# A graph kernel's half stage loads 133 of a row's 325 columns

## What is computed

```python
out_i = act(jnp.concatenate([x_i, edge_attr], -1) @ W).reshape(-1, HEADS, DIM)
out_j = act(jnp.concatenate([x_j, edge_attr], -1) @ W).reshape(-1, HEADS, DIM)
alpha = act((jnp.concatenate([out_i, out_j], -1) * att).sum(-1))
mu = alpha.mean(0)
var = alpha.var(0)
alpha = (alpha - mu) * jax.lax.rsqrt(var + BN_EPS) * bn_gamma + bn_beta
alpha = act(alpha)
alpha = segment_softmax(alpha, i, N_NODES)
msg = out_j * alpha[:, :, None]
aggr = jax.ops.segment_sum(msg, i, num_segments=N_NODES)
out = aggr.mean(1) + bias
```

## Time and profile before

| | |
|---|---|
| median of 3 runs | 6269.24 us (6267.83 to 6273.7) |
| profiled execution, its own time | 6264.56 us |
| its span in the trace | 6262.9 us |
| PE busy | 4644.9 us (74%) |
| DVE busy | 4803.2 us (77%) |
| ACT busy | 3989.2 us (64%) |
| POOL busy | 3785.3 us (60%) |
| moved by DMA | 1270.97 MB |

### The profile page before, as it was taken

One profiled execution on the slowest core, in us unless ns is written; L12 is line 12 of the kernel. 1 busy time (PEld: TensorE's weight loads), 2 busy tenths in 40 slices (PEclk: granted clock), 3 DMA queues, 4 the chain that ended last, 5 costly groups with the idle time before them and its releaser, 6 DMA issues. The chain is left out here.

```text
span 6262.9 us, 166674 instructions
## 1 busy us (share of the span) xinstructions
PE 4644.9 (74%) x32887; PEld 3061.9 (49%) x32888; DVE 4803.2 (77%) x30826; ACT 3989.2 (64%) x10577; POOL 3785.3 (60%) x5381
## 2 busy tenths in 40 slices
PE   1367766777666666578988988889838888886799
PEld 0144444444343343345555555555425555554799
DVE  6588988888887788678888888888876677667233
ACT  3366666666555555478888888888867777776000
POOL 2277777777776666645555555555547777776000
PEclk8599999998888888799999999999979999998899
DMA  8767767676555555566556666556537777774798
GB/s 217 251 221 229 229 220 231 217 231 205 195 189 196 189 187 186 185 193 166 165 165 166 169 165 165 166 164 166 144 107 216 216 216 217 215 217 147 298 361 340
DMA packets 913988, 1270.97 MB, mean 203 GB/s; under 512 B 268468, under 2 KB 775459, under 8 KB 894916
## 3 DMA queue, kind: packets, MB, share of 16 engines
q1 hardware_dynamic: 785592, 864.14, 47.7%
q0 software_dynamic: 88560, 320.26, 13.8%
q10 hardware_dynamic: 39580, 84.01, 3.6%
HBM read 837.45 MB, written 430.64 MB: 202 GB/s over the span
## 5 line engine op out<-in xcount | busy, mean ns | idle before, releaser
L912 POOL DMA_INDIRECT rows<-rowS,idx x1616 | 1754.8, 1086 | 614.5 <-issue 478.3
L1632 POOL TENSOR_SCALAR one<-io128b,bufh 128x128 bf16<-128x128 bf16 x912 | 716.3, 785 | 796.2 <-DMA bufh<-rows 796.1
L1666 DVE CUSTOM_DVE_ANT_0 junk<-bufh,attb 128x64 bf16<-128x64 f32 x5472 | 1021.6, 233 | 150.3 <-ACT bufh L1714 134.2
L1172 PE MATMUL psa<-one_c,one_s 128*128 128x392 bf16 x2352 | 552.7, 347 | 733.2 <-DVE one_s L994 501.5
L2397 PE MATMUL psm<-msg,onem 128*128 128x260 f32 x3648 | 919.9, 395 | 211.5 <-issue 177.1
L2318 POOL TENSOR_TENSOR msg<-oj,heads 128x512 f32<-128x512 f32 x760 | 796.2, 1069 | 211.6 <-DMA oj<-rows 177.3
L2397 PEld LDWEIGHTS psm<-msg,onem 128*128 128x128 f32 x3648 | 648.7, 190 | 482.4 <-issue 407.4
L986 DVE TENSOR_TENSOR one_c<-ioc,pairS 128x1176 bf16<-128x1176 f16 x784 | 593.9, 757 | 245.5 <-DMA pairS<-pairs 127.2
L1754 PE MATMUL pre<-P3h,oneT 128*128 x5472 | 756.5, 274 | 0.0
L1008 DVE CUSTOM_DVE_ANT_0 weighed<-rowS,att_row 128x64 bf16<-128x64 f32 x4848 | 735.6, 214 | 7.6 <-ACT rowS L1068 7.5
L1065 ACT ACTIVATE lgS<-preS 128x1024 f32<-128x1024 f32 x404 | 413.2, 1023 | 440.1 <-PE preS L1161 439.3
(11 more groups left out here) (306 smaller groups left out, 9161.8 us busy)
## 6 DMA issues: line engine op xcount, KB each, us to landing
bufh<-rows SPq DMA_DIRECT2D x912, 325.0 KB, 3.3
oj<-rows SPq DMA_DIRECT2D x912, 256.0 KB
adj<-adj SPq DMA_DIRECT2D x70, 1568.0 KB, 9.4
adj<-cnts ACTq DMA_DIRECT2D x49, 1568.0 KB, 7.2
eaS<-in_edge_attr_dram SPq DMA_DIRECT2D x201, 256.0 KB
low<-dlow SPq DMA_DIRECT2D x202, 252.0 KB
adj_early<-adj SPq DMA_DIRECT2D x28, 1568.0 KB, 8.5
rows<-blanktail POOLq DMA_DIRECT2D x20, 1625.0 KB, 44.0
```

What stands on the lines that cost most here:

```text
L912: eng.indirect_dma_start(out=m["rows"][h], out_offset=bass.IndirectOffsetOnAxis(ap=idx[s][:, k:k + 1], axis=0), in_=rows[s][:, k, :], in_o ...
L1172: mm = eng.matmul(psa[r][:, 0:z.GC], one_s[r][:, k, :], one_c[r][:, k, :], start=(k == 0), stop=(k == GT - 1))
L1632: eng.tensor_scalar(one[j % PRE][:, 1, :], m["io128b"][:, :], buf[j][:, 1, 0, LANE:LANE + 1], 0.0, ALU.add, ALU.is_equal).then_inc(second_ ...
L1666: ins = eng.tensor_tensor_reduce(junk[q][:, k * H + h, 0, :], buf[j][:, k, 1, h * D:(h + 1) * D], attb[:, 1, h, :], 1.0, 0.0, ALU.mult, AL ...
```

## The change

The load of the half stage takes columns DOTS * D = 192 to 325 of each row in place of all 325, and puts them at the same place in the buffer. Columns 0 to 191, the first three heads of `out_j`, are left out; their dot products come with the row. The number of transfers, the semaphores, the buffers and the order of instructions on every engine stay the same, and the rows in DRAM too.

```diff
@@ -1617,7 +1617,7 @@
             def body(i, h):
                 for j in range(BU):
                     wait(eng, sp_read[j], i)
-                    eng.dma_start(buf[j][:, :, 0, :], tiles(i, j, h)).then_inc(row_in[j], 16)
+                    eng.dma_start(buf[j][:, :, 0, DOTS * D:RW], tiles(i, j, h)[:, :, DOTS * D:RW]).then_inc(row_in[j], 16)
 
             paired_parts(eng, z.its, body)
```

## The result

The changed kernel takes 6166.7 us in the median of 4 runs (6164.8 to 6175.18), the kernel before 6268.53 (4 runs beside them, 6261.71 to 6273.7). The ratio is 0.9841, 95% interval 0.9824 to 0.9858: 1.6% faster. The profiled execution took 6167.14 us of its own time (span 6165.4), 97.4 less than that of before.

What follows compares the result with a forecast made beforehand. The half stage was bound by a ring of load, POOL, PE, ACT and DVE, with one DMA latency per pass. 152 passes x 0.62 = 94 us; 6264.6 - 94 = 6170.6, set at 6173; range 6130 to 6221 us.

Steps and rivals of the forecast that it cites:

- One DMA latency per pass: Half stage: a load's 3.26 us wait lies on the path once per six-unit pass, not once per unit.
- The cut of 0.66 us: Half stage load: engine time falls from 1.21 to 0.55 us, landing to 2.6 to 2.65 us.
- the ring: Half stage: load, POOL, PE, ACT and DVE wait on each other over six buffers, 11.59 us in the pass read.
- The cap of 0.67 us or a little over: Half stage: the most a pass can give, however fast the load, before DVE's half of the one-hot decides.
- DVE's ring: Half stage: DVE's in-order sums, one-hots and reads with PE and ACT; would leave a pass of 10.92 us.
- the tie: Half stage: cut 0.66 and cap 0.67 us leave two rings level, the later deciding each time.
- The 0.62 us per pass: Half stage: gain taken per pass after cut and cap; over 152 passes 94 us.
- Rival E: Half stage: earlier POOL work slows DVE's reads, making the kernel slower, 125 us, 6390 us; 5%.
- A: Half stage load: smaller cut, 0.74 us of engine time per load, 46 to 71 us gained; 17%.
- B: Half stage: gain hidden anyway, DVE's half as late as POOL's; no change, 6264 to 6270 us; 10%.
- C: Half stage: larger cut, 0.89 us, with DVE's slack; 0.75 to 0.9 us per pass, 114 to 137 us gained; 13%.
- D: Half stage: gain partly eaten as earlier POOL work meets DVE's reads, 10 to 45 us gained; 5%.

Runs made afterwards that it cites:

- wide_early: Kernel before, full 325-column load kept; DVE reads the fourth head first, so SP issues the next load earlier: 6684.53 us against 6838.92, ratio 0.9785.
- small_early: Changed kernel (133 columns), with DVE reading the fourth head first so the load is issued earlier: 6669.85 us, ratio 0.9758 to the kernel before.
- tally: Changed kernel, with DVE making the one-hot of a pass's unit 3 ahead of adding up the old pass's sums: 6124.68 us, ratio 0.9813 to the kernel before.
- mid: Kernel before, with only the first head's 64 columns left out of the load (261 columns): 6791.64 us, ratio 0.9948.
- tiny: Changed kernel, loading only 69 columns, the fourth head's part left out and zeros in its place: 6108.65 us, ratio 0.9785 to the kernel before.

## Why the prediction was right

- **One DMA latency per pass: right.** Landing and stage time go together over four kernels that differ only in the load: 3.3 us and 1833; 3.0 and 1791; 2.5 and 1736; 2.2 and 1686. That is 147 us for 1.05 us (3.27 to 2.22 at two decimals), 0.92 us per pass for each us of landing. And wide_early gives the same kind of gain with no byte less.
- **The cut of 0.66 us: right for the ring, too small for the landing.** The engine time fell by 1.21 - 0.56 = 0.65 us, the value taken. The median landing fell by 0.74, to 2.52 and not 2.6 to 2.65. What the ring feels is POOL's start: from the issue to it the mean fell from 3.43 to 2.75 us, by 0.69. By the Trainium skill's fit (DMA: Bandwidth & Descriptors, Anatomy of one DMA) it would have been 0.45, and these runs don't bear that out: its 69 us stand against 97. The page gives that fit for transfers that GpSimd issues, which the prediction did not say; these loads are issued by SP.
- **The cap of 0.67 us or a little over: wrong as a mean.** It is true of the pass that I read, 11.59 us, one of the shortest: only 5% of the passes take 11.6 us or less. The mean pass had 12.06. The floor of DVE's ring is small_early's 1672 / 152 = 11.0 us, so the cap was 1.06 us per pass. The error was to take a cap from one pass and the gain from the mean of all. With it went the tie: the load's ring went on leading, by 0.29 us in the mean and in 94% of the passes.
- **The 0.62 us per pass: 0.636 measured, in part by luck.** The prediction took 0.66 and put off 0.04 for two tied rings. The rings did not tie. In the table the load's step gave 0.69, and small losses that the sum did not have took it back to 12.07 - 11.45 = 0.62: 0.04 in POOL's one-hot (0.79 to 0.83), 0.04 from PE's transpose to Exp, 0.02 ahead of the issue, less 0.03 in the last steps. The errors of the cut (0.03) and of the tie (0.04) met these losses (0.06).
- **Rival E's mechanism is there, but did not grow.** In the kernel before, DVE's read of one head takes 236 ns where POOL works beside nearly all of it and 215 where POOL stands still (2043 and 1872 reads in passes 10 to 149); in the changed kernel 233 and 218. POOL's one-hot of any unit took 0.72 us where no read lay beside it and 0.80 where reads lay beside more than 80% of it. So both pay a little, and neither is held up for the length of the other. This agrees with the rule that stood beside it (the Trainium skill, SBUF — State Buffer, Who interferes with whom), that this pair contends. What did grow, POOL's one-hot of unit 0, was not pushed into reads by the change, it lay among them before; why it grew stays open. It now lies beside DVE's one-hot of the same unit for 0.30 us where that was 0.06, and DVE's one-hot grew with it, from 0.25 to 0.31 us; in small_early the two don't meet and it takes 0.25, in tally they meet for 0.33 and it takes 0.34.
- **Rivals.** A is out (a load takes 0.56 us of engine time, not 0.74), B is out (mid and tiny move the time by the load alone), C is out by its cut (it needed 0.75 to 0.89 us and the load's step gave 0.69; the true cap would have allowed it). D and E are out in size.

## What to carry to other kernels

Where each load waits for its buffer's last reader and the next product waits for the load, as here, a ring of buffers puts one transfer's latency on the path once per trip of the ring. Both a shorter transfer and an earlier issue cut it; the earlier issue, which frees the part of a buffer that the load overwrites as soon as its last reader is through, was worth more here (152 us) than dropping 59% of the bytes (97). Take a cap from the same mean over passes as the gain, never from one pass that happens to be clean.

## What the hardware showed that I had not expected

The landing of a load shrank by more than its engine time: by 0.74 us for 0.65, and by 0.30 us more for 276-byte runs, whose engine time is 0.185 x 1687 / 906 = 0.34 us, 0.22 less. Shorter runs went on costing less: per packet, semaphores included, 71 ns at 1300 bytes, 33 at 532 and 20 at 276. And a DVE read and POOL's one-hot side by side each take about a tenth longer: 236 ns against 215 for the read, 0.80 us against 0.72 for the one-hot, in the kernel before.
